# A two-layer state-space kernel: scratch copies in 4 KB pieces, rows of B loaded ahead of C, product 3 of the second scan on POOL, and two statistics moved on DVE

## The chip, the cores and the metric

The kernel runs on one core of one Trainium2 chip. The metric is the device time of one execution in microseconds. A profiled execution comes with a trace: every instruction of TensorE (PE, with its weight loads PEld), VectorE (DVE), ScalarE (ACT) and GpSimd (POOL), the DMA issues of SyncE (SP) and POOL, and the clock granted to TensorE. All data is float32.

## The reference

Four stages, each `x = layernorm(x + f(x))`, on 4096 tokens of 256 channels. The first `f` is a Mamba-2 layer (chunked scan), the second a small coupling network applied three times. The change lies mostly in the third and fourth:

```
xz = x @ w_in.T + b_in;  x_ssm, z = split(xz);  z = silu(z)
dt = softplus(x_ssm @ w_dt.T + b_dt)
Bm, Cm = x_ssm @ w_B.T + b_B, x_ssm @ w_C.T + b_C          # 16 states each
A = -exp(A_log)                                            # (256 channels, 16 states)
for each token t, channel d, state n:
    h[d,n] = exp(A[d,n] * dt[t,d]) * h[d,n] + dt[t,d] * Bm[t,n] * x_ssm[t,d]
    y[t,d] = sum over n of h[d,n] * Cm[t,n]
y = ((y + D * x_ssm) * z) @ w_out.T + b_out
x1 = layernorm(y + x) * gamma + beta;  x = layernorm(x + x1)
h = layernorm(x) * ln_gamma + ln_beta
x = layernorm(x + x + 0.5 * (silu(h @ w1 + b1) @ w2 + b2)) # w1, w2 from integers times scales
```

The text of the reference writes the last two lines with `residual = x`; the kernel joins the normalizations into scales and shifts, which is why there are "norm 3", "norm 4 and 5" and "norm 6".

## The kernel before, in words

**Stages.** Up to some 330 us runs the Mamba-2 layer, up to some 520 us the coupling network, and then the scan stage, which is the third and the fourth stage together. Tokens are worked in 8 blocks of 512. In the scan stage channels lie on the 128 partitions, two tiles of 512 tokens side by side (2 x 512 elements a partition).

**One state of one block** takes these steps (`n` is the state, 0 to 15; `k` the half of the channels):
- SP loads row `n` of B (`load_B`, L1620) and of C (`load_C`, L1626) from the scratch tensor `CB_rows`, spread over all partitions: 256 KB in pieces of 2 KB. There are four buffers for each. The loads wait for an earlier use of their buffer.
- POOL multiplies `dt*x` by the row of B (`into`, L2560; "input n" in the text).
- ACT makes the decay `exp(A*dt)` in PSUM, once for each half (`decay`, L2021).
- DVE runs the scan over 512 tokens, once for each half (`scan`, L2343).
- ACT saves the last column for the next block (`carry`, L2032) and copies the row of C into a PSUM bank, of which there is one (`spread_C`, L2027). DVE multiplies state and C (`product`, L2350). For the states in `on_pool` (0, 12 and 14) POOL multiplies instead, straight from the loaded row (L2570), and ACT makes no copy.
- PE transposes the product and adds it up over the states (`add_up`, L1762).

**Order.** Each engine works through a list written out by hand, one iteration `it` for each block, with the names `cur` (block `it`), `post` (`it-1`), `last` (`it-2`), `old` (`it-3`). DVE scans states 8 to 15 of a block in the iteration after the one that scans 0 to 7. Semaphores alone tie the engines together; an instruction that waits holds all behind it on its engine. SP's list holds the loads too: a load that waits holds the ones behind it.

**Between the scans** the same lists hold the rest of the blocks before: the gated output is transposed and projected; DVE adds the residual `x2` to it (`residual`, L2362) and takes statistics (`stats3`, L2369, two halves); POOL turns them into scale and shift (`norm3`, `norm36`, L2592 and L2600; `norm36` does norm 6 of an older block with it); ACT applies them; POOL multiplies by gamma (`scaled`, L2632) and adds `x2 + beta` (`summed`, L2637); DVE takes the second statistics (`stats4`, L2374); POOL makes norm 4 and 5 of them (`norm45`, L2605); ACT applies them; PE and ACT run the two layers of the feed-forward network. `x2 + beta` is made by a DMA of POOL that adds beta, spread over partitions, onto the buffer of `x2` (`shifted`, L2577). ACT also prepares the next block: `evac_x`, `evac_d` and, behind the decays of states 8 and the first of 9, `soft_step` (L2056), which needs another function table.

**Scratch.** The second stage stores its result twice, as tokens (`x2_tokens`, L1094) and as channels (`x2_rows`, L1103); the scan stage loads blocks of them again (`load_x2`, L1607, and `load_xT`, L1602), and `load_x2` stands on SP behind B 2. The token form moves in pieces of 1 KB, the channel form in pieces of 2 KB; beta moves in pieces of 1 KB.

Of the kernel before, what the change touches and what calls it, by code (L numbers as in the profile page):

```python
# [43 lines left out]
def build(nc, d, out, scratch):  # L44
    with ExitStack() as ctx:
# [967 lines left out]
        x2_tokens, x2_rows = scratch["x2_tokens"].rearrange("(n p) f -> p n f", p=P), rows(scratch["x2_rows"])  # L1013
# [7 lines left out]
        def coupling():  # L1021
# [66 lines left out]
            def sync(e, early_loads):  # L1088
# [3 lines left out]
                for b in range(NB):  # L1092
                    e.wait_ge(c_n, 4 * b + 4)
                    e.dma_start(x2_tokens[:, b * NC:(b + 1) * NC, :], x2s[b % 2][:, :, :]).then_inc(c_tok[b % 2], DMAS)  # L1094
# [8 lines left out]
                    e.dma_start(x2_rows[:, :, tokens(b)], x1T[:, :, tokens(b)]).then_inc(c_row, DMAS)  # L1103
# [424 lines left out]
        with ExitStack() as pd:  # L1528
# [12 lines left out]
            beta_row = d["everywhere"].rearrange("(a o n) -> a o n", a=1, o=1)[:, :, sum(n for _, n in EVERYWHERE) - DM:]  # L1541
# [34 lines left out]
            p_g, on_pool = d_sem("p_g"), (0, 12, 14)  # L1576
# [24 lines left out]
            def sync(e):  # L1601
                def load_xT(b):  # L1602
                    e.wait_ge(pe_z, 2 * b)
                    e.wait_ge(c_row, DMAS * (b + 1))
                    e.dma_start(xT[:, :, :], x2_rows[:, :, b * TB:(b + 1) * TB]).then_inc(ld_xT, DMAS)

                def load_x2(b):  # L1607
# [6 lines left out]
                    e.dma_start(x2, x2_tokens[:, b * NC:(b + 1) * NC, :]).then_inc(ld_x2, DMAS)  # L1614
# [34 lines left out]
                for it in range(NB + 3):  # L1649
                    old, post, cur, nxt = it - 3, it - 1, it, it + 1  # L1650
                    if live(post):
# [7 lines left out]
                        load_C(post, 13)  # L1659
                    if 0 < cur < NB:  # L1660
                        store_CB(cur)
# [8 lines left out]
                    if live(post):  # L1670
                        load_x2(post)
# [10 lines left out]
                    if live(cur):  # L1682
# [4 lines left out]
                        load_B(cur, 7)  # L1687
                        load_C(cur, 6)
                        load_B(cur, 8)
                        load_C(cur, 7)  # L1690
                        load_B(cur, 9)
                        load_C(cur, 8)
                        load_B(cur, 10)
# [326 lines left out]
            def scalar(e):  # L2020
# [130 lines left out]
                for it in range(NB + 3):  # L2151
# [124 lines left out]
                    if live(cur):  # L2276
                        decay(cur, 4, 1)
                        spread_C(cur, 3)
# [63 lines left out]
            def vector(e):  # L2342
# [116 lines left out]
                for it in range(NB + 3):  # L2459
# [4 lines left out]
                    if live(post):  # L2464
                        scan(post, 8, 0)
# [3 lines left out]
                    if live(post):  # L2469
                        product(post, 7)  # L2470
# [46 lines left out]
                    if 0 <= post < NB - 1:  # L2517
                        residual(post, 1)
                        stats3(post, 0)
                    if live(cur):  # L2520
                        scan(cur, 3, 0)
                        scan(cur, 3, 1)
                    if 0 <= post < NB - 1:
                        stats3(post, 1)
                    if live(cur):
                        product(cur, 2)
                    if live(cur):
                        scan(cur, 4, 0)
                        scan(cur, 4, 1)
                        product(cur, 3)  # L2530
# [28 lines left out]
            def pool(e):  # L2559
# [17 lines left out]
                def shifted(b):  # L2577
                    e.wait_ge(v_pre, 2 * b + 2)
                    e.dma_start(x2, beta_row.to_broadcast([P, NC, DM]), accum_op=ALU.add).then_inc(ld_beta, DMAS)
# [209 lines left out]
```

## Time and profile before

| | us |
|---|---|
| median of 3 runs | 1088.25 |
| lowest, highest | 1087.13, 1093.55 |
| profiled execution, its own time | 1091.2 |
| span of its trace | 1089.2 |
| busy PE, PEld, DVE | 980.9, 743.0, 929.0 |
| busy ACT, POOL | 839.4, 709.3 |
| granted TensorE clock, mean | 0.966 |

The page cuts the span into 40 equal slices of 27.2 us and gives the busy share of each in tenths:

```profile
DVE  7999999999963797865799898999999899999751
POOL 2556566766761111223789899999999899999530
PEclk9999999999998999999877799999999999999999
DMA  6543435433415002112998968588786978678301
```

The scan stage begins in slice 20. A row of the time line gives start, duration, engine, line, operation, what is written and read, and in brackets the idle time before it with its releaser. Neighbouring starts on DVE lie closer than the durations say, since an instruction starts while the one before it drains.

### The profile page before, as it was taken

How to read it: one execution, taken by the hardware profiler on the slowest of the kernel's cores; microseconds unless marked ns; L12 is line 12 of the kernel's file. 1: busy time of each engine (PE TensorE's matmuls, PEld its weight loads, DVE VectorE, ACT ScalarE, POOL GpSimd, SP SyncE). 2: the span in 40 equal slices, each digit the busy share in tenths (PEclk: the TensorE clock that was granted, in tenths of full speed). 3: DMA queues.
4: the chain of work that ended last, by engine and by line, in shares of the span. 5: the costliest groups of instructions: out<-in, count | busy, mean ns of one | idle time of the engine just before them, and what ended most of it. 6: DMA issues, size and time to landing. Idle time of an engine off the chain costs nothing. (4 is left out here: it accounts for less than half of the span.)

```text
span 1089.2 us, 17899 instructions
## 1 busy us (share of the span) xinstructions
PE 980.9 (90%) x5612; PEld 743.0 (68%) x5612; DVE 929.0 (85%) x1234; ACT 839.4 (77%) x1633; POOL 709.3 (65%) x603
## 2 busy tenths in 40 slices
PE   6999999999978999998668499999999989997987
PEld 4777777777754555555446387777778777886776
DVE  7999999999963797865799898999999899999751
ACT  7778878878746668767877789898998988987733
POOL 2556566766761111223789899999999899999530
PEclk9999999999998999999877799999999999999999
DMA  6543435433415002112998968588786978678301
GB/s 178 145 134 116 135 110 141 122 99 111 126 46 195 0 1 75 43 39 85 244 163 185 141 152 183 129 199 158 162 169 162 168 133 192 171 146 170 86 1 39
DMA packets 97617, 137.53 MB, mean 126 GB/s; under 512 B 8818, under 2 KB 52338, under 8 KB 97524
## 3 DMA queue, kind: packets, MB, share of 16 engines
q1 hardware_dynamic: 93828, 132.73, 50.2%
q0 software_dynamic: 3696, 3.67, 2.8%
q8 instruction: 45, 0.74, 0.3%
q14 instruction: 48, 0.39, 0.2%
HBM read 120.12 MB, written 14.16 MB: 123 GB/s over the span
## 5 line engine op out<-in xcount | busy, mean ns | idle before, releaser
L2348 DVE TENSOR_TENSOR_SCAN oa<-bank_a,h,oa 128x512 f32<-128x512 f32 x128 | 159.8, 1269 | 13.6 <-ACT h L2034 9.7
L2348 DVE TENSOR_TENSOR_SCAN ob<-bank_a,h,ob 128x512 f32<-128x512 f32 x128 | 160.0, 1268 | 8.0 <-ACT bank_a L2025 4.5
L1830 PE MATMUL bank_m<-w,f_h 128*128 128x256 f32 x448 | 104.4, 383 | 0.0
L1491 POOL TENSOR_TENSOR oa<-ob,x1T 128x1024 f32<-128x1024 f32 x8 | 18.8, 2355 | 130.5 <-DVE ob L1391 130.5
L2025 ACT ACTIVATE bank_a<-s,A 128x512 f32<-128x512 f32 x128 | 86.7, 683 | 21.2 <-DVE oa L2348 15.1
L2025 ACT ACTIVATE bank_a<-dtc,A 128x512 f32<-128x512 f32 x128 | 87.0, 684 | 13.7 <-DVE oa L2348 8.1
L1830 PEld LDWEIGHTS bank_m<-w,f_h 128*128 128x128 f32 x448 | 84.4, 192 | 14.1 <-issue 3.6
L1770 PE MATMUL bank_y<-ident,ob 128*128 128x128 f32 x512 | 71.7, 286 | 23.2 <-DVE ob L2354 11.8
L1770 PE MATMUL bank_y<-ident,oa 128*128 128x128 f32 x512 | 72.3, 288 | 17.7 <-DVE oa L2354 17.6
L1770 PEld LDWEIGHTS bank_y<-ident,ob 128*128 128x128 f32 x512 | 62.7, 148 | 34.5 <-DVE ob L2354 14.5
L2568 POOL TENSOR_TENSOR ob<-s,Bb 128x1024 f32<-128x1024 f32 x32 | 76.1, 2378 | 15.0 <-DMA Bb<-CB_rows 10.9
L1770 PEld LDWEIGHTS bank_y<-ident,oa 128*128 128x128 f32 x512 | 63.0, 149 | 29.1 <-DVE oa L2354 21.2
L2568 POOL TENSOR_TENSOR ob<-uc,Bb 128x1024 f32<-128x1024 f32 x32 | 76.1, 2377 | 10.2 <-DMA Bb<-CB_rows 6.5
L673 DVE TENSOR_TENSOR_SCAN L<-abc,zeros,b_id 128x512 f32<-128x512 f32 x64 | 78.3, 1265 | 4.6 <-POOL xd L883 3.6
L2568 POOL TENSOR_TENSOR oa<-uc,Bb 128x1024 f32<-128x1024 f32 x32 | 76.1, 2378 | 9.0 <-DMA Bb<-CB_rows 4.4
L883 POOL TENSOR_TENSOR xd<-xs,L 128x512 f32<-128x512 f32 x32 | 34.0, 1062 | 72.4 <-DVE xs L662 71.9
L2568 POOL TENSOR_TENSOR oa<-s,Bb 128x1024 f32<-128x1024 f32 x32 | 76.1, 2377 | 3.3 <-POOL ob L2575 2.1
L2354 DVE TENSOR_TENSOR oa<-ob,bank_c 128x1024 f32<-128x1024 f32 x64 | 77.3, 1207 | 0.9
L2030 ACT ACTIVATE bank_c<-Cb 128x512 f32<-128x512 f32 x104 | 61.6, 592 | 13.2 <-DVE ob L2354 8.2
L334 PE MATMUL b_op<-W_out,zs 128*128 128x256 f32 x256 | 63.1, 389 | 0.0
L2575 POOL TENSOR_TENSOR ob<-oa,Cb 128x1024 f32<-128x1024 f32 x24 | 57.2, 2383 | 2.7 <-PE bank_y L1770 2.7
L640 DVE SCALAR_TENSOR_TENSOR b_p<-raw,columns,b_p 128x512 f32<-128x512 f32 x72 | 54.2, 753 | 3.3 <-ACT b_p L465 1.7
(405 smaller groups left out, 2912.7 us busy)
## 6 DMA issues: line engine op xcount, KB each, us to landing
Bb<-CB_rows SPq DMA_DIRECT2D x128, 256.0 KB, 6.6
Cb<-CB_rows SPq DMA_DIRECT2D x128, 256.0 KB, 6.4
abc<-decays SPq DMA_DIRECT2D x32, 512.0 KB, 4.5
Ebc<-ramps SPq DMA_DIRECT2D x64, 128.0 KB, 3.1
uT<-in_uT SPq DMA_DIRECT2D x8, 512.0 KB, 4.2
u<-in_u SPq DMA_DIRECT2D x8, 512.0 KB, 3.9
x_tokens<-x2s SPq DMA_DIRECT2D x8, 512.0 KB, 3.2
x_rows<-x1T SPq DMA_DIRECT2D x8, 512.0 KB, 3.0
```

The lines of the kernel that those rows point to most:

```text
L334: i = e.matmul(b_op[:, 0:DM], zs[b % 2][:, m, ts], W_out[:, m, :], start=(m == 0), stop=(m == MD - 1))
L640: e.scalar_tensor_tensor(to, raw[:, m, t:t + TB], cw[:, m, t:t + 1], acc[:, :], ALU.mult, ALU.add).then_inc(v_conv, 1)
L673: e.tensor_tensor_scan(L[:, hs, :].rearrange("p h t -> p (h t)"), abc[g % 2][:, hs, :].rearrange("p h t -> p (h t)"), b_id[:, :], zeros[:, ...
L883: e.tensor_tensor(heads(xd[:, :]), heads(xs[g % 2][:, :]), L[:, :, CH - 1:CH].to_broadcast([P, NH, HD]), ALU.mult).then_inc(p_xd, 1)
L1770: i = e.matmul(p_y[c // 2][:, at:at + P], prod[n % 2][:, k, c * CH:(c + 1) * CH], ident[:, :], start=False, stop=(n == NS - 1), is_transpo ...
L1830: i = e.matmul(to, f_h[:, k, c * CH:(c + 1) * CH], w2[:, k, :], start=False, stop=(c % 2 == 1 and k == KF - 1))
L2025: e.activation(p_a[k][:, :], dtc[b % 2][:, k, :], ACT.Exp, scale=A[:, k, n:n + 1]).then_inc(a_a, 1)
L2030: e.activation(p_c[:, :], Cb[n % 4][:, :], ACT.Copy).then_inc(a_c, 1)
L2348: e.tensor_tensor_scan(s[:, k, :], p_a[k][:, :], s[:, k, :], h0[:, n, k:k + 1], ALU.mult, ALU.add).then_inc(v_s, 1)
L2354: e.tensor_tensor(prod[n % 2][:, :, :], state[(NS * b + n) % 4][:, :, :], both(p_c[:, :]), ALU.mult).then_inc(v_g, 1)
L2568: e.tensor_tensor(state[at % 4][:, :, :], uc[b % 2][:, :, :], both(Bb[n % 4][:, :]), ALU.mult).then_inc(p_b, 1)
L2575: e.tensor_tensor(prod[n % 2][:, :, :], state[(NS * b + n) % 4][:, :, :], both(Cb[n % 4][:, :]), ALU.mult).then_inc(p_g, 1)
```

## The change

- `x2_tokens`, `x2_rows` are laid out by partition and block, so that stores and loads of a block move 4 KB to or from a partition in one piece. Beta is repeated four times in an input of its own (`beta_rows`), so that its load moves 4 KB a partition too.
- On SP `load_x2` goes ahead of the store of B and C of the next block; B 8 goes ahead of C 6, B 9 ahead of C 7, B 10 ahead of C 8.
- State 3 joins `on_pool`: its product goes from DVE (and the copy from ACT) to POOL, between norm 3 and input 6. With it C 7 waits for POOL's product.
- On DVE both `stats4` go ahead of scan 8's first half, and the second `stats3` ahead of both halves of scan 3.
- On POOL `summed` and `norm45` go one input earlier each.

```
-        x2_tokens, x2_rows = scratch["x2_tokens"].rearrange("(n p) f -> p n f", p=P), rows(scratch["x2_rows"])
+        x2_tokens, x2_rows = scratch["x2_tokens"], scratch["x2_rows"]
-   e.dma_start(x2_tokens[:, b * NC:(b + 1) * NC, :], x2s[b % 2][:, :, :]).then_inc(c_tok[b % 2], DMAS)
+   e.dma_start(x2_tokens[:, b, :], x2s[b % 2][:, :, :].rearrange("p c f -> p (c f)")).then_inc(c_tok[b % 2], DMAS)
-   e.dma_start(x2_rows[:, :, tokens(b)], x1T[:, :, tokens(b)]).then_inc(c_row, DMAS)
+   e.dma_start(x2_rows[:, b, :, :], x1T[:, :, tokens(b)]).then_inc(c_row, DMAS)
-   beta_row = d["everywhere"].rearrange("(a o n) -> a o n", a=1, o=1)[:, :, sum(n for _, n in EVERYWHERE) - DM:]
+   beta_row = d["beta_rows"].rearrange("(a n) -> a n", a=1)
-   p_g, on_pool = d_sem("p_g"), (0, 12, 14)
+   p_g, on_pool = d_sem("p_g"), (0, 3, 12, 14)
-   e.dma_start(xT[:, :, :], x2_rows[:, :, b * TB:(b + 1) * TB]).then_inc(ld_xT, DMAS)
+   e.dma_start(flat(xT), x2_rows[:, b, :, :].rearrange("p k t -> p (k t)")).then_inc(ld_xT, DMAS)
-   e.dma_start(x2, x2_tokens[:, b * NC:(b + 1) * NC, :]).then_inc(ld_x2, DMAS)
+   e.dma_start(flat(x2), x2_tokens[:, b, :]).then_inc(ld_x2, DMAS)
@@ SP
                         load_C(post, 13)
+                        load_x2(post)
                     if 0 < cur < NB:
                         store_CB(cur)
...
                         load_B(cur, 2)
-                    if live(post):
-                        load_x2(post)
...
                         load_B(cur, 7)
+                        load_B(cur, 8)
                         load_C(cur, 6)
-                        load_B(cur, 8)
+                        load_B(cur, 9)
                         load_C(cur, 7)
-                        load_B(cur, 9)
+                        load_B(cur, 10)
                         load_C(cur, 8)
-                        load_B(cur, 10)
                         load_B(cur, 11)
@@ ACT
                         decay(cur, 4, 1)
-                        spread_C(cur, 3)
                         carry(cur, 3)
@@ DVE
-                    if live(post):
-                        scan(post, 8, 0)
                     if 0 <= last < NB - 1:
                         stats4(last, 0)
                         stats4(last, 1)
                     if live(post):
+                        scan(post, 8, 0)
                         product(post, 7)
...
                         stats3(post, 0)
+                        stats3(post, 1)
                     if live(cur):
                         scan(cur, 3, 0)
                         scan(cur, 3, 1)
-                    if 0 <= post < NB - 1:
-                        stats3(post, 1)
-                    if live(cur):
                         product(cur, 2)
                     if live(cur):
                         scan(cur, 4, 0)
                         scan(cur, 4, 1)
-                        product(cur, 3)
                         scan(cur, 5, 0)
@@ POOL
-   e.dma_start(x2, beta_row.to_broadcast([P, NC, DM]), accum_op=ALU.add).then_inc(ld_beta, DMAS)
+   e.dma_start(flat(x2), beta_row.to_broadcast([P, NC * DM]), accum_op=ALU.add).then_inc(ld_beta, DMAS)
                     if live(cur):
+                        product(cur, 3)
                         into(cur, 6)
                         into(cur, 7)
                         into(cur, 8)
                     if 0 <= post < NB - 1:
                         scaled(post)
+                        summed(post)
                     if live(cur):
                         into(cur, 9)
                     if 0 <= post < NB - 1:
-                        summed(post)
+                        norm45(post)
                     if live(cur):
                         into(cur, 10)
-                    if 0 <= post < NB - 1:
-                        norm45(post)
-                    if live(cur):
                         into(cur, 11)
@@ inputs and scratch
+        "beta_rows": np.tile(a[L1 + "beta"], NC),
-    ("x2_tokens", (T, DM)), ("x2_rows", (DM, T))
+    ("x2_tokens", (P, NB, NC * DM)), ("x2_rows", (P, NB, KD, TB))
```

## Rows read from the trace of the kernel before

**Rows 1.** Busy us (x instructions) of each engine in one stretch, clock, DMA:
```profile
750.00:825.00 75.00, 70.06 (x422) 57.44 (x422) 72.28 (x73) 67.39 (x123) 70.32 (x43) 1.00 0.82 169
```

**Rows 2.** Time line of DVE: the product of state 9 in blocks 0 to 4
```profile
561.76 1.20 DVE L2354 TENSOR_TENSOR oa<-ob,bank_c 128x1024 f32<-128x1024 f32 x1
...
624.54 1.20 DVE L2354 TENSOR_TENSOR oa<-ob,bank_c 128x1024 f32<-128x1024 f32 x1
...
689.26 1.22 DVE L2354 TENSOR_TENSOR oa<-ob,bank_c 128x1024 f32<-128x1024 f32 x1
...
752.69 1.21 DVE L2354 TENSOR_TENSOR oa<-ob,bank_c 128x1024 f32<-128x1024 f32 x1
...
816.11 1.21 DVE L2354 TENSOR_TENSOR oa<-ob,bank_c 128x1024 f32<-128x1024 f32 x1
```

**Rows 3.** Time line of DVE, block 4: scan 4, product 3, scans 7, 8, statistics, 9
```profile
790.05 2.56 DVE L2348 TENSOR_TENSOR_SCAN oa<-bank_a,h,oa 128x512 f32<-128x512 f32 x2 [1.44 <-ACT h L2034]
792.54 1.20 DVE L2354 TENSOR_TENSOR oa<-ob,bank_c 128x1024 f32<-128x1024 f32 x1
...
803.36 1.28 DVE L2348 TENSOR_TENSOR_SCAN ob<-bank_a,h,ob 128x512 f32<-128x512 f32 x1 [0.35 <-POOL ob L2568]
804.55 1.27 DVE L2348 TENSOR_TENSOR_SCAN oa<-bank_a,h,oa 128x512 f32<-128x512 f32 x1
805.74 1.29 DVE L2376 BATCH_NORM_STATS2 st<-xl 128x6 f32<-128x512 f32 x2
...
811.06 1.28 DVE L2348 TENSOR_TENSOR_SCAN ob<-bank_a,h,ob 128x512 f32<-128x512 f32 x1 [0.54 <-ACT bank_a L2025]
```

**Rows 4.** Time line of ACT, block 4: evac_x, spread_C 4, decays 7 and 9
```profile
792.70 0.69 ACT L2041 ACTIVATE xc<-bank_m,columns 128x512 f32<-128x512 f32 x1 [0.27 <-PE bank_m L40]
...
793.83 0.60 ACT L2030 ACTIVATE bank_c<-Cb 128x512 f32<-128x512 f32 x1 [0.35 <-DVE oa L2354]
...
802.55 0.67 ACT L2025 ACTIVATE bank_a<-dtc,A 128x512 f32<-128x512 f32 x1
...
805.86 0.69 ACT L2025 ACTIVATE bank_a<-dtc,A 128x512 f32<-128x512 f32 x1 [0.18 <-DVE oa L2348]
```

**Rows 5.** Time line of DVE: the second statistics of blocks 0 and 4
```profile
616.36 1.30 DVE L2376 BATCH_NORM_STATS2 st<-xl 128x6 f32<-128x512 f32 x2 [4.85 <-POOL xl L2641]
...
871.75 1.31 DVE L2376 BATCH_NORM_STATS2 st<-xl 128x6 f32<-128x512 f32 x2 [2.50 <-POOL xl L2641]
```

**Rows 6.** Time line of POOL, block 4: input 5, beta's DMA, input 7, sum
```profile
784.09 2.38 POOL L2568 TENSOR_TENSOR ob<-uc,Bb 128x1024 f32<-128x1024 f32 x1 [0.92 <-DMA Bb<-CB_rows]
786.40 1.34 POOL L2579 DMA_DIRECT2D s<-in_everywhere  x1
...
793.90 2.37 POOL L2568 TENSOR_TENSOR ob<-uc,Bb 128x1024 f32<-128x1024 f32 x1 [1.14 <-DVE oa L2354]
...
803.21 2.38 POOL L2641 TENSOR_TENSOR xl<-xl,s 128x1024 f32<-128x1024 f32 x1
```

**Rows 7.** Time line of SP's queue, block 1: the issue of B 9
```profile
597.49 0.79 SPq L1624 DMA_DIRECT2D Bb<-CB_rows  x1
```

**Rows 8.** Time line of POOL, block 1: inputs 3 and 9
```profile
585.87 2.36 POOL L2568 TENSOR_TENSOR ob<-s,Bb 128x1024 f32<-128x1024 f32 x1 [1.40 <-DMA Bb<-CB_rows]
...
611.68 2.34 POOL L2568 TENSOR_TENSOR ob<-s,Bb 128x1024 f32<-128x1024 f32 x1 [3.42 <-DMA Bb<-CB_rows]
```

**Rows 9.** Busy us by stretch, as rows 1; the clock is the third number from the end
```profile
615.00:630.00 15.00, 8.48 (x51) 7.22 (x52) 12.86 (x12) 9.23 (x19) 13.82 (x15) 0.54 0.95 152
```

**Rows 10.** Time line of POOL, block 0: input 6
```profile
541.16 2.39 POOL L2568 TENSOR_TENSOR oa<-uc,Bb 128x1024 f32<-128x1024 f32 x1
```

**Rows 11.** DMA queues from 786 to 800 us: packets, MB, share of 16 engines
```profile
q1 hardware_dynamic: 998, 1.81, 61.7%
q0 software_dynamic: 528, 0.52, 33.7%
```

**Rows 12.** Beta's DMA, all seven: us from its issue to its landing
```profile
DMA to landing us min/median/max: 10.0/11.5/15.9
```

More of the change, by code:

```diff
@@ L1012, in build @@
         ld_B, ld_C = [d_sem(f"ld_B{i}") for i in range(4)], [d_sem(f"ld_C{i}") for i in range(4)]
-        x2_tokens, x2_rows = scratch["x2_tokens"].rearrange("(n p) f -> p n f", p=P), rows(scratch["x2_rows"])
+        x2_tokens, x2_rows = scratch["x2_tokens"], scratch["x2_rows"]
         c_row, c_tok = new_sem("c_row"), [new_sem("c_tok0"), new_sem("c_tok1")]
@@ L1539, in both @@
                 return x.rearrange("p (o t) -> p o t", o=1).to_broadcast([P, KD, TB])
-            beta_row = d["everywhere"].rearrange("(a o n) -> a o n", a=1, o=1)[:, :, sum(n for _, n in EVERYWHERE) - DM:]
+            beta_row = d["beta_rows"].rearrange("(a n) -> a n", a=1)
             def rowwise(v):
@@ L1659, in sync @@
                         load_C(post, 13)
+                        load_x2(post)
                     if 0 < cur < NB:
@@ L1687, in sync @@
                         load_B(cur, 7)
+                        load_B(cur, 8)
                         load_C(cur, 6)
-                        load_B(cur, 8)
+                        load_B(cur, 9)
                         load_C(cur, 7)
-                        load_B(cur, 9)
+                        load_B(cur, 10)
                         load_C(cur, 8)
-                        load_B(cur, 10)
                         load_B(cur, 11)
@@ L2469, in vector @@
                     if live(post):
+                        scan(post, 8, 0)
                         product(post, 7)
@@ L2519, in vector @@
                         stats3(post, 0)
+                        stats3(post, 1)
                     if live(cur):
@@ L2701, in pool @@
                     if live(cur):
+                        product(cur, 3)
                         into(cur, 6)
                         into(cur, 7)
-                    if live(cur):
                         into(cur, 8)
@@ L2707, in pool @@
                         scaled(post)
+                        summed(post)
                     if live(cur):
@@ L2778 @@
         "columns": np.concatenate([column(down[n]) for n, _ in COLUMNS], axis=1),
+        "beta_rows": np.tile(a[L1 + "beta"], NC),
         "everywhere": np.concatenate([every[n].reshape(-1) for n, _ in EVERYWHERE]),
@@ L2784 @@
     out = nc.dram_tensor("out", (T, DM), F32, kind="ExternalOutput").ap()
-    scratch = {n: nc.dram_tensor(n, shape, F32, kind="Internal").ap() for n, shape in (("x2_tokens", (T, DM)), ("x2_rows", (DM, T)), ("CB_rows", (2 * NS, T)), ("decays", (NB * NC, DT, CH)), ("ramps", (NB * NC, DT, CH)))}
+    scratch = {n: nc.dram_tensor(n, shape, F32, kind="Internal").ap() for n, shape in (("x2_tokens", (P, NB, NC * DM)), ("x2_rows", (P, NB, KD, TB)), ("CB_rows", (2 * NS, T)), ("decays", (NB * NC, DT, CH)), ("ramps", (NB * NC, DT, CH)))}
     build(nc, dram, out, scratch)
```

26 lines of the change are left out of this document (7 added, 19 removed).

## The prediction

> **What bounds the kernel now.** The page's row of forty slices comes first: DVE stands at 8 to 9 tenths through most of the last half, the scan stage (from 520 us), and every edit but the layout of two scratch stores lies there. In a steady stretch DVE is busy 72.3 us of 75, POOL 70.3 and ACT 67.4 [rows 1]: three engines near full, so a microsecond taken from one counts only if the other two leave room. The pace of a block is read from DVE's product of state 9, which comes once a block: 62.8, 64.7, 63.4 and 63.4 us from one to the next [rows 2]. The third view is DVE, ACT and POOL in order of time through one block. It shows a loop that DVE's busy share hides. The first half of scan 8 ends at 805.8; only then may ACT run the first decay of state 9, and behind that, in ACT's order, stand a table load, the softplus of the next block and another table load. Then comes the second decay of state 9, for which DVE waits 0.54 us at 811.06 [rows 3, 4]. From 805.86 to 811.06 are 5.2 us. The last view is the waits of DVE: for POOL it waits long only twice, 4.85 and 2.50 us, both ahead of the second normalization's statistics [rows 5].
>
> **The sum is made** for the profiled execution, 1091.2 us with a span of 1089.2; the median of the three runs is 1088.25, so 2.95 less.
>
> **Product 3 leaves DVE** in all 8 blocks: 1.20 us by its row, 1.1 from its start to the next [rows 3]; ACT loses the copy of C for it, 0.6 us like the one at 793.83. At most that is 8 x 1.1 = 9 us. How much arrives is read on ACT. The lost copy stood ahead of the second x evacuation, which waits for PE until 792.70 anyway [rows 4], so its removal moves nothing behind that. What ACT gains comes later: the copy of C 4 no longer waits 0.35 us for product 3. From there ACT runs without a gap through both norms and the decays to that of state 7 at 802.55, which the scan at 803.36 has to have [rows 3, 4]. So I take 0.45 us a block, the copy moving from 793.83 to 793.38; the ends are 0 and 1.1.
>
> **Product 3 enters POOL** behind the first norm, 2.38 us. It waits for nothing there: scan 3 is over by 787.4 (790.05 less the wait of 1.44 and product 2), and POOL is at this point at 790.4 (793.90 less 1.14 and one input of 2.35). The 1.14 us that POOL waited for product 3 ahead of input 7 [rows 6] go away. The sum ahead of input 9 takes 2.33 us from the way to the second statistics, what the product puts in. POOL ended the sum at 805.6 (803.21 + 2.38); less 1.14 that is 804.45, and less the wait of 0.92 for a row of B [rows 6], if it goes, 803.5. DVE would be done with scan 7 at 804.05 (805.74, less scan 8's 1.2, less 0.45). So both arrive together, and I take 0.2 us of new waiting, in one block; the second norm then ends before input 10, which is wanted 3 us later still.
>
> **Statistics ahead of scan 8.** Both, 1.2 us, now delay the first half of scan 8 and with it the whole ACT loop of 5.2 us. DVE filled that loop with the statistics, product 7 and two scans (4.7 us); now with 3.5. The wait at 811.06 grows by 1.2. Against it stands the 0.45: **+0.7 us in a steady block**. If ACT gains nothing it is +1.2, if all 1.1 arrive +0.1. The last block has no softplus behind it: -0.5. The other pair of statistics goes ahead of scan 3; ACT is late there until 790.05 by 1.44 us [rows 3] whatever DVE's order, so that costs 0, and 0.6 if this cover were gone.
>
> **B ahead of C, x2 earlier.** C 7 now waits on SP for POOL's product 3 (end 792.8); behind it stand B 10, C 8, B 11, the output store and C 9. B 10 and B 11 must wait for inputs 6 and 7 in any case (795.1 and 797.5), and are used only behind the sum: free. B 9 comes ahead of C 7 and leaves when input 5 ends (786.4), 6 us earlier. In block 1 B 9 left at 597.49 [rows 7] and input 9 began at 611.68 after 3.42 us of idle [rows 8]: 14.1 us of landing. Issued at 595.5 it is there at 609.6, before it is wanted. The x2 load, put where SP waits for ACT anyway, clears the way for B 3, which cost 1.40 us [rows 8]. POOL then ends block 1's sum at 612.5 (616.36 less 3.42 and, in part, 1.40 with beta's landing), but now the ACT loop follows that the stall had hidden: second half of scan 9 at 612.5 + 2.4 + 5.2 = 620.1, was 616.36 + 4.7 = 621.1. That is -1.0 and not -4.9. Block 5 in the same way: 867.6 + 2.4 + 5.2 = 875.2, was 871.75 + 4.7 = 876.5: -1.3.
>
> **Clock.** Behind the 4.85 us stall PE was granted 0.54 of full speed from 615 to 630, near its 1.2 GHz level [rows 9], and block 2 took 64.7 us where 63.4 are usual [rows 2]. With a shorter stall I expect it to stay up: block 2 is -1.3 + 0.7 = -0.6; the other end is +0.7.
>
> **Block 0** has no normalization yet, and POOL is just ahead of DVE. Input 6 starts at 541.16 [rows 10], and behind product 3 at 543.5; scan 6 follows 1.3 us later than today. +1.3, at the low end 0.
>
> **4 KB pieces.** The loads of x2 and xT and the two stores are off the path. Of the beta load the row shows 528 pieces, 0.52 MB, that hold 33.7% of the engines' 14 us, while 998 pieces and 1.81 MB of the other queue hold 61.7% [rows 11]: 4.7 us of all 16 engines, at the other queue's bytes per time 2.5. It leaves at 786.4 and is now wanted at 802.1, 15.7 us later; it lands after 11.5 us in the median, 15.9 at most [rows 6, 12]. POOL's own 1.34 us to issue it may fall (0 to 1.34 less). I take 0 for all of this, as nothing of it is waited for. The Trainium skill (DMA: Bandwidth & Descriptors, Queues, rings and completion order) says that each DMA engine changes between its queues a packet at a time, by which larger beta packets would push the rows of B back. No run here shows a 4 KB piece yet; by that rule B 8, with 14.2 us to spare, would at the worst landing of 14.1 plus beta's 4.7 be 4.6 us late once, and the sum would come to 1093.
>
> **Sum:** +1.3 (block 0) - 1.0 (1) - 0.6 (2) + 0.7 x 3 (3, 4, 6) + 0.2 - 1.3 (5) - 0.5 (7) = +0.2 us. Forecast: **no change**, 1091.4 for a profiled execution and 1088.5 for the median.
>
> **Rivals.** *A, the loop is not tight.* ACT has some slack behind scan 8 that the order of the rows does not show, and the wait there does not grow. Then the stalls pay in full: +1.3 - 3.9 (1) - 1.8 (2) - 0.5 x 3 - 3.8 (5) - 0.5 (7) = -10.2, so 1078; with the whole 1.1 of each product 1073. For it: DVE is the fullest engine and loses an instruction, and its wait at 811.06 is only 0.54 us. Chance 0.22, of which 0.14 lies beyond 1%.
> *B, the beta load becomes the wait; slower.* The sum now wants beta 15.7 us after its issue, and from that point each microsecond is DVE's, since statistics, scan 8 and the ACT loop stand behind it. The 15.9 us of one landing speaks for it, the median of 11.5 against. With landings of 17.7 us in the 6 middle blocks it costs 6 x 2 = 12: 1100.5. Chance 0.08.
> *C, the loads stay jammed.* Another row comes late in B 9's stead, and blocks 1 and 5 gain nothing, nor does the clock: +1.3 + 0 + 0.7 x 5 - 0.5 = +4.3, so 1092.5. For it: 14.1 us for one row of 256 KB is congestion, not order. Chance 0.16.
> The forecast itself has 0.54.
>
> **Range and chances.** The forecast's own bounds are 4 us to either side: below, ACT lets all of the 1.1 through in 6 blocks; above, it lets nothing through and the clock dips again. With C and the nearer part of A the range is 1077 to 1096; outside lie B and the far part of A. About 1% (11 us) is what a measurement of this kernel can tell from no change: faster 0.14, same 0.78, slower 0.08.
>
> **What would show it.** Right: DVE's wait ahead of scan 9's second half grows from 0.54 to about 1.7; no 4.85 or 2.50 ahead of the statistics; DVE busy 9 to 10 us less, POOL 19 more; steady products of state 9 64.1 us apart. Wrong: that wait still near 0.5 (A); POOL idle ahead of the sum, released by the beta load (B); POOL idle ahead of inputs 6 to 9 for rows of B (C).

## The result, and the profile after

| | before | after |
|---|---|---|
| median of 20 executions each, us | 1091.7 | 1094.38 |
| lowest, highest | 1087.13, 1094.82 | 1091.59, 1097.03 |
| profiled execution: its own time, span | 1091.2, 1089.2 | 1091.81, 1090.0 |
| busy DVE, POOL, ACT | 929.0, 709.3, 839.4 | 920.8, 723.9, 835.0 |

The ratio of after to before is 1.0035, with a 95% interval of 1.0023 to 1.0047: slower by a third of a per cent, well inside 1%, but the interval lies clear of 1. (The ratio is estimated from the single executions; the two medians alone give 1.0025.) DVE lost 8.2 us of work and the kernel gained nothing by it.

The page of the changed kernel, its slices and its DMA queues:

```profile
DVE  7999999999963897965799898999989999999751
POOL 3456466766761111323889999999999999999530
DMA  5443434433415002113996668487676657667201
...
q1 hardware_dynamic: 86788, 132.73, 47.0%
q0 software_dynamic: 1008, 3.67, 1.7%
```

In the last half DVE's slices are much as before, and POOL's are almost all nines: the work that left DVE is on POOL. The answer to [rows 1], the same 75 us:

```profile
750.00:825.00 75.00, 69.01 (x412) 55.88 (x412) 70.66 (x71) 66.13 (x120) 71.08 (x43) 1.00 0.73 170
```

DVE is busy 1.6 us less and POOL 0.8 us more; the DMA share fell from 0.82 to 0.73. Where DVE's time went is seen in block 4, in DVE's time line (the answer to [rows 3]: scans 4 and 7, statistics, scan 8, product 7, scan 9):

```profile
791.00 2.56 DVE L2346 TENSOR_TENSOR_SCAN oa<-bank_a,h,oa 128x512 f32<-128x512 f32 x2 [1.44 <-ACT h L2033]
...
803.84 1.28 DVE L2346 TENSOR_TENSOR_SCAN ob<-bank_a,h,ob 128x512 f32<-128x512 f32 x1
805.03 1.29 DVE L2374 BATCH_NORM_STATS2 st<-xl 128x6 f32<-128x512 f32 x2
806.23 1.27 DVE L2346 TENSOR_TENSOR_SCAN oa<-bank_a,h,oa 128x512 f32<-128x512 f32 x1
807.42 1.21 DVE L2352 TENSOR_TENSOR oa<-ob,bank_c 128x1024 f32<-128x1024 f32 x1
...
812.74 1.28 DVE L2346 TENSOR_TENSOR_SCAN ob<-bank_a,h,ob 128x512 f32<-128x512 f32 x1 [1.75 <-ACT bank_a L2024]
```

and in ACT's, the answer to the last of [rows 4]:

```profile
807.54 0.69 ACT L2024 ACTIVATE bank_a<-dtc,A 128x512 f32<-128x512 f32 x1 [1.39 <-DVE oa L2346]
808.25 1.28 ACT L2057 ACT_TABLE_LOAD   x1
809.55 1.06 ACT L2057 ACTIVATE s<-s 128x1024 f32<-128x1024 f32 x1
810.62 1.28 ACT L2024 ACT_TABLE_LOAD   x1
811.91 0.69 ACT L2024 ACTIVATE bank_a<-dtc,A 128x512 f32<-128x512 f32 x1
```

Scan 8's first half starts at 806.23, behind the statistics. ACT has been idle for 1.39 us for it. Then ACT runs decay, table load, softplus, table load and decay without a gap, and DVE, whose filling is 1.2 us shorter, waits 1.75 us where it waited 0.54. The waits of DVE from 520 us on (total, times, longest) show that this is now the largest within the blocks; only two waits at the very end of the kernel, together 16.8 us and as long before, come to more. Seven of the eight are this wait, one in each of blocks 0 to 6, 1.72 or 1.75 us long; the one in block 0 is as long before the change, and the eighth is one of 0.93 in block 2:

```profile
DVE ob L2346 <- ACT bank_a L2024: 13.2, 8, 1.8
DVE oa L2346 <- ACT h L2033: 9.8, 6, 2.6
```

Block 4 is 64.16 us long by the start of scan 9's second half (748.58 to 812.74), where it was 63.4. What the stalls gave back is seen in block 1 on DVE (the answer to the first of [rows 5]; the second has no wait any more). The statistics there are of block 0's tokens, but they stand in the stretch in which DVE works on states 8 to 15 of block 1, and are called those of block 1 from here on; those of [rows 5] at 871.75 are those of block 5 in the same way:

```profile
612.18 1.30 DVE L2374 BATCH_NORM_STATS2 st<-xl 128x6 f32<-128x512 f32 x2 [2.39 <-POOL xl L2635]
...
619.89 1.28 DVE L2346 TENSOR_TENSOR_SCAN ob<-bank_a,h,ob 128x512 f32<-128x512 f32 x1 [1.75 <-ACT bank_a L2024]
```

The wait for POOL fell from 4.85 to 2.39 us, and the one for ACT's loop, which the long stall had hidden, came behind it. POOL in block 4 (the answer to [rows 6]: beta's DMA, product 3, sum, input 9):

```profile
786.34 0.95 POOL L2573 DMA_DIRECT2D s<-in_beta_rows  x1
...
790.49 2.35 POOL L2569 TENSOR_TENSOR oa<-ob,Cb 128x1024 f32<-128x1024 f32 x1 [0.58 <-PE bank_y L1769]
...
802.37 2.37 POOL L2635 TENSOR_TENSOR xl<-xl,s 128x1024 f32<-128x1024 f32 x1 [0.20 <-POOL xl L2629]
804.70 2.36 POOL L2562 TENSOR_TENSOR ob<-uc,Bb 128x1024 f32<-128x1024 f32 x1
```

The sum ends at 804.7 and DVE begins the statistics at 805.03, without a wait. Beta's DMA takes POOL 0.95 us instead of 1.34, and over its seven issues it lands after 10.1 us at least, 10.8 in the median and 12.2 at most:

```profile
DMA to landing us min/median/max: 10.1/10.8/12.2
```

### The profile page after: what moved, and what is told of

Its sections match the earlier page's. It is cut to its first block and busy times, and to the rows that moved or that the text cites. A ratio compares the mean times of both kernels' runs of the same rounds, so it can differ in the third digit from the quotient of the medians.

```text
span 1090.0 us, 17891 instructions
## 1 busy us (share of the span) xinstructions
PE 979.1 (90%) x5612; PEld 740.8 (68%) x5612; DVE 920.8 (84%) x1226; ACT 835.0 (77%) x1625; POOL 723.9 (66%) x611
## 5 line engine op out<-in xcount | busy, mean ns | idle before, releaser
L1769 PEld LDWEIGHTS bank_y<-ident,oa 128*128 128x128 f32 x512 | 62.8, 149 | 26.2 <-DVE oa L2352 18.1
L2352 DVE TENSOR_TENSOR oa<-ob,bank_c 128x1024 f32<-128x1024 f32 x56 | 67.8, 1211 | 3.5 <-PE bank_y L1769 2.6
L2029 ACT ACTIVATE bank_c<-Cb 128x512 f32<-128x512 f32 x96 | 56.9, 593 | 11.4 <-DVE ob L2352 9.3
```

The costliest lines, as they stand in the source:

```text
L1769: i = e.matmul(p_y[c // 2][:, at:at + P], prod[n % 2][:, k, c * CH:(c + 1) * CH], ident[:, :], start=False, stop=(n == NS - 1), is_transpo ...
L2029: e.activation(p_c[:, :], Cb[n % 4][:, :], ACT.Copy).then_inc(a_c, 1)
L2352: e.tensor_tensor(prod[n % 2][:, :, :], state[(NS * b + n) % 4][:, :, :], both(p_c[:, :]), ALU.mult).then_inc(v_g, 1)
```

## The experiments

"Steady block" is the distance between the same instructions of two neighbouring blocks, 3 and 4 or 4 and 5, on DVE. Before it is 63.4 us, after 64.15. The first four experiments share one set of executions of the kernel before (28), the next four another (26), the last three a third (12). A number in brackets is a number of executions. Steady blocks of one kernel agree within 0.06 us; blocks 0 and 1 don't. The loads alone and the filled loop on top of them have the same order of instructions up to scan 9 of block 1, and the pieces alone and their filled version too. Yet block 0 takes 37.9 and 41.8 us in the first two, and block 1 takes 58.6 and 62.0 in the others. So one profile can't price a change in these two blocks to better than some 3 us.

**Scan 8 first.** The changed kernel, with only the order of scan 8 and the statistics as before:

```
@@ DVE, changed kernel
+                    if live(post):
+                        scan(post, 8, 0)
                     if 0 <= last < NB - 1:
                         stats4(last, 0)
                         stats4(last, 1)
                     if live(post):
-                        scan(post, 8, 0)
                         product(post, 7)
```

> The changed kernel with one edit undone: on DVE the first half of scan 8 stands ahead of the second statistics again. Theory L (the ACT loop from scan 8 through the softplus to scan 9 sets the pace): DVE's wait ahead of scan 9's second half falls from 1.75 back to about 0.55 us, steady blocks take 63.0 us instead of 64.15, and the time is some 7 us below the changed kernel: 1087 to 1088, ratio to before about 0.996. Rival P (POOL with its fourth product is the bound): POOL's work is untouched, so blocks stay at 64.1 and the ratio at 1.0035.

1091.76 us (12 executions) against 1093.32 for the kernel before (28), ratio 0.9988, interval 0.9974 to 1.0003. DVE, then POOL behind the sum, in the steady block:

```profile
810.34 1.28 DVE L2346 TENSOR_TENSOR_SCAN ob<-bank_a,h,ob 128x512 f32<-128x512 f32 x1 [0.55 <-ACT bank_a L2024]
```

```profile
803.55 2.37 POOL L2563 TENSOR_TENSOR ob<-uc,Bb 128x1024 f32<-128x1024 f32 x1
806.50 0.20 POOL L2603 TENSOR_SCALAR ve<-st 128x4 f32<-128x4 f32 x1 [0.58 <-DVE st L2374]
```

The wait for ACT is back at 0.55, so the order of scan 8 and the statistics is what had made it 1.75. But the block is 63.43 us and not 63.0, and the ratio not 0.996 as expected. POOL is now the bound: it is busy 60.56 of 63.43 us, what is left are its own gaps of 0.2 to 0.4 us, and it has a new wait of 0.58 us. With norm 4 and 5 one input earlier, POOL reaches them before DVE has finished the statistics.

**Product 3 back on DVE.** The changed kernel with this one edit undone:

```
-            p_g, on_pool = d_sem("p_g"), (0, 3, 12, 14)
+            p_g, on_pool = d_sem("p_g"), (0, 12, 14)
@@ ACT
+                        spread_C(cur, 3)
@@ DVE
+                        product(cur, 3)
@@ POOL
-                        product(cur, 3)
```

> The changed kernel with product 3 back on DVE and its copy back on ACT; the order of the statistics and all loads stay as changed. Theory L: the loop stays and the 0.45 us that the moved product gave each block is lost: blocks of 64.3 to 64.6 us, ratio to before 1.004 to 1.007. Rival P: POOL loses 19 us of work, so blocks fall to 63.4 us and the ratio to 0.998 to 1.000.

1094.37 us (12) against 1093.32, ratio 1.0018, interval 1.0001 to 1.0035. The steady block:

```profile
806.58 1.29 DVE L2375 BATCH_NORM_STATS2 st<-xl 128x6 f32<-128x512 f32 x2
...
814.29 1.28 DVE L2347 TENSOR_TENSOR_SCAN ob<-bank_a,h,ob 128x512 f32<-128x512 f32 x1 [1.75 <-ACT bank_a L2024]
```

The wait is 1.75 us with product 3 on either engine, and the block is 64.62 us against 64.15. So the move of the product is worth 0.47 us a block here, though it takes 1.2 us from DVE. In the whole it is worth nothing that can be told: the ratio of 1.0018 is below the 1.004 to 1.007 that was expected, and the median is 1094.37 us with the product on DVE and 1094.38 with it on POOL. One place where the gain is lost is block 1: with the product on DVE there is no wait ahead of the statistics at 613.23, with it on POOL there is one of 2.39 us.

**The statistics' order alone,** in the kernel before:

```
@@ DVE, kernel before
-                    if live(post):
-                        scan(post, 8, 0)
                     if 0 <= last < NB - 1:
                         stats4(last, 0)
                         stats4(last, 1)
                     if live(post):
+                        scan(post, 8, 0)
                         product(post, 7)
```

> The kernel before with one edit of the change alone: the second statistics ahead of scan 8 on DVE; POOL keeps its order, so its sum ends at the old place, 1.1 us after DVE is ready for the statistics. Theory L: 1.2 us from the longer loop plus 1.1 us of waiting for the sum, some 2.3 us in each of 6 blocks: blocks of 65.7 us, ratio about 1.012. Rival P: the order of two short DVE instructions costs nothing that POOL does not hide, ratio 1.000 to 1.001.

1114.17 us (6) against 1093.32, ratio 1.0189, interval 1.0162 to 1.0215. The steady block is 65.69 us. In DVE's time line the second wait is in block 4, and the third belongs to the stall of [rows 5]:

```profile
814.55 1.31 DVE L2376 BATCH_NORM_STATS2 st<-xl 128x6 f32<-128x512 f32 x2 [0.99 <-POOL xl L2640]
...
822.27 1.28 DVE L2348 TENSOR_TENSOR_SCAN ob<-bank_a,h,ob 128x512 f32<-128x512 f32 x1 [1.75 <-ACT bank_a L2025]
...
884.01 1.31 DVE L2376 BATCH_NORM_STATS2 st<-xl 128x6 f32<-128x512 f32 x2 [3.01 <-POOL xl L2640]
```

This order costs 2.3 us a block by itself: 1.2 in ACT's loop, and 1.0 because the sum on POOL is not ready when DVE wants it. The steady block came as expected; the whole was more than the expected 1.012. Part of that is that a wait for POOL ahead of the statistics is now paid in full, since the loop stands behind it: block 5 takes 69.5 us and not 65.4. Another 3.4 us of this profile are in block 0, where this edit moves nothing; its cause is open.

**All edits of the loads alone,** in the kernel before: 4 KB pieces, `load_x2` earlier, rows of B ahead of C.

```
@@ SP, kernel before with the pieces of 4 KB
+                        load_x2(post)
...
+                        load_B(cur, 8)
                         load_C(cur, 6)
-                        load_B(cur, 8)
+                        load_B(cur, 9)
                         load_C(cur, 7)
-                        load_B(cur, 9)
+                        load_B(cur, 10)
...
```

> The kernel before with the transfers' part alone: the 4 KB pieces, the x2 load earlier, rows of B ahead of C. Theory D (order and pieces end the two stalls): the waits of 4.85 and 2.50 us for the sum go to 1 and 0 us, the rest of the blocks stays at 63.4 us; against the profiled execution of before that is 6 us less, against a median whose runs may have had smaller stalls 2 to 6: ratio 0.994 to 0.998. Rival N (the loads were hidden, the stalls a matter of the execution): ratio 1.000 within 0.001, stalls somewhere else.

1088.37 us (11) against 1093.32, ratio 0.9955, interval 0.9940 to 0.9971. The steady block is 63.41 us as before, and the stall of block 1 is nearly gone:

```profile
613.61 1.32 DVE L2375 BATCH_NORM_STATS2 st<-xl 128x6 f32<-128x512 f32 x2 [0.42 <-POOL xl L2640]
```

The loads, with their pieces, are the useful part of the change.

**The pieces alone,** in the kernel before: the layout of the two scratch tensors and of beta, SP's order untouched (the listing is cut to the loads of `x2` and beta).

```
-   e.dma_start(x2, x2_tokens[:, b * NC:(b + 1) * NC, :]).then_inc(ld_x2, DMAS)
+   e.dma_start(flat(x2), x2_tokens[:, b, :]).then_inc(ld_x2, DMAS)
-   e.dma_start(x2, beta_row.to_broadcast([P, NC, DM]), accum_op=ALU.add).then_inc(ld_beta, DMAS)
+   e.dma_start(flat(x2), beta_row.to_broadcast([P, NC * DM]), accum_op=ALU.add).then_inc(ld_beta, DMAS)
```

> The kernel before with the 4 KB pieces alone; every load stands in its old place. Theory O (the order of the rows ended the stalls): input 9 of blocks 1 and 5 still waits 1 to 3 us for its row of B, DVE still waits 1 to 5 us for the sum there, ratio 0.999 to 1.000. Theory S (the size did it, as beta and x2 hold the DMA engines for a shorter time): no wait above 1 us for the sum, ratio 0.9955 as with both.

1088.21 us (11) against 1091.44 (26), ratio 0.9964, interval 0.9947 to 0.9981. Block 1 on DVE, and POOL's input 9 and sum ahead of it:

```profile
611.45 1.32 DVE L2376 BATCH_NORM_STATS2 st<-xl 128x6 f32<-128x512 f32 x2
```

```profile
606.71 2.36 POOL L2568 TENSOR_TENSOR ob<-s,Bb 128x1024 f32<-128x1024 f32 x1
609.03 2.36 POOL L2641 TENSOR_TENSOR xl<-xl,s 128x1024 f32<-128x1024 f32 x1
```

POOL goes from input 9 to the sum with no wait for a row of B, with B 9 still behind C 7 on SP. Its issue, the answer to [rows 7]:

```profile
597.38 0.71 SPq L1624 DMA_DIRECT2D Bb<-CB_rows  x1
```

It landed 7.4 us after this; issued at 597.49 in the kernel before, it took 14.0. The size of the pieces ended the stalls, not the order of the rows. Block 5's stall is gone too. Which of the three it was, beta, `x2` or the channel form, was not tried one by one. The profiled execution, 1085.25 us, was among the quickest of its eleven, so its gain of 6 us is not the kernel's.

**Scan 8 first, norm 4 and 5 where they were.** The first experiment, and on POOL:

```
@@ POOL, on top of "scan 8 first"
+                    if live(cur):
+                        into(cur, 10)
                     if 0 <= post < NB - 1:
                         norm45(post)
                     if live(cur):
-                        into(cur, 10)
                         into(cur, 11)
```

> The kernel with scan 8 ahead of the statistics (e1), and on POOL the second norm behind input 10 again, where it was before the change. In e1 blocks took 63.4 us with POOL never idle but for waits on the statistics of up to 0.6 us. Theory W (the loop is gone and POOL, which waits for the statistics inside its own chain, is the next bound): that wait goes, blocks take 62.9 to 63.0 us, the 1.68 us ahead of scan 10 in the last block goes as well, and the time is 3 to 6 us below e1: ratio to before 0.993 to 0.996. Rival P (POOL's pure work is the bound): blocks stay at 63.4 and the ratio at 0.998 to 0.999.

1088.29 us (10) against 1091.44, ratio 0.9972, interval 0.9958 to 0.9986: a smaller gain than the 0.993 to 0.996 that was expected, though the steady block is as expected, 62.98 us. POOL no longer waits for the statistics:

```profile
805.97 2.37 POOL L2563 TENSOR_TENSOR oa<-uc,Bb 128x1024 f32<-128x1024 f32 x1
808.43 0.20 POOL L2603 TENSOR_SCALAR ve<-st 128x4 f32<-128x4 f32 x1
```

Against the loads alone (63.41) this is 0.43 us a block for product 3, with the earlier sum and `stats3` that go with it. What it gained there it lost in the first blocks: statistics of block 1 at 615.0 with a wait of 1.14 us, where the loads alone have 613.61 and 0.42.

**The loop filled,** with all edits of the loads in the kernel before. DVE gets the feed-forward's last sums of an older block ahead of the instruction that waits for ACT:

```
@@ DVE, kernel before with the loads
-                        scan(post, 9, 1)
-                        product(post, 8)
                     if 0 <= old < NB - 2:
                         second(old, 0)
+                    if live(post):
+                        scan(post, 9, 1)
+                        product(post, 8)
```

> The kernel before with the transfers' part (e4), and on DVE the first half of the feed-forward sum (two instructions, 0.8 us) moved from behind product 8 to between the two halves of scan 9, where DVE waits 0.54 us for ACT. Theory L: the wait is filled, blocks take 62.9 us and not 63.41, the time is some 2.5 us below e4: ratio to before 0.993. Rival: the instruction now waits for PE's down projection, or ACT is the bound all round, and blocks stay at 63.4 with the ratio at 0.9955.

1086.42 us (5) against 1091.44, ratio 0.9949, interval 0.9930 to 0.9969. Only the steady block shows the gain over the loads alone; the ratios, 0.9949 and 0.9955, can't be told apart. The wait of 0.54 is gone and the steady block is 62.76 us, 0.65 less and a little better than expected:

```profile
807.40 1.26 DVE L2347 TENSOR_TENSOR_SCAN ob<-bank_a,h,ob 128x512 f32<-128x512 f32 x1
808.57 0.84 DVE L2381 SCALAR_TENSOR_TENSOR x3b<-xl,twice,bank_m 128x256 f32<-128x256 f32 x2
809.34 1.27 DVE L2347 TENSOR_TENSOR_SCAN ob<-bank_a,h,ob 128x512 f32<-128x512 f32 x1
```

**The two together:** scan 8 first, norm 4 and 5 later, product 3 on POOL, and the loop filled with the same edit.

> e5 and the filled loop together: product 3 on POOL, scan 8 ahead of the statistics, second norm behind input 10, the feed-forward sum inside scan 9. Theory W: DVE alone would allow 62.5 us, POOL's own work 62.8 to 62.9, so blocks take about 62.9 us and little is left of the filled loop: within 1 us of e5. If DVE or ACT were still the bound: 62.4 to 62.5 us, some 3 us below e5.

1087.44 us (11) against 1091.44, ratio 0.9962, interval 0.9947 to 0.9977. Without the filled loop it was 1088.29, so this is within the 1 us that was expected. The steady block is 62.93 us, 0.17 more than with product 3 left on DVE. POOL is busy 60.56 us of it, with gaps of 0.2 to 0.4 us between dependent steps, and DVE, which has room now, waits for POOL's input instead:

```profile
772.74 1.28 DVE L2346 TENSOR_TENSOR_SCAN ob<-bank_a,h,ob 128x512 f32<-128x512 f32 x1 [0.87 <-POOL ob L2564]
```

So product 3 on POOL is worth 0.47 or 0.43 us a block while ACT's loop binds DVE, and less than nothing once it doesn't. That is read from the steady blocks; the whole times of the last two kernels (0.9962 and 0.9949) can't be told apart.

**Pieces and filled loop, without the order of the loads,** the same edit on the pieces alone:

> Before with the 4 KB pieces alone, and the second half of scan 9 with product 8 behind the feed-forward's sums, so that DVE has work while ACT is in its loop. Theory S (the size of the pieces ended the stalls, the order of the loads adds nothing): steady blocks 62.8 us apart, no wait over 0.4 us ahead of scan 9's second half, no stall over 0.5 us ahead of the second statistics, ratio to before 0.992 to 0.996, the same as with x2 and the rows of B moved too. Theory O (the order is needed as soon as DVE is quicker): blocks of over 63.0 or a stall of over 1 us for POOL ahead of the second statistics, ratio 0.996 or more.

1085.67 us (8) against 1091.72 (12), ratio 0.9945, interval 0.9923 to 0.9967, with steady blocks of 62.76 us and no stall ahead of the second statistics of block 1. Theory S holds, but for a wait of 0.54 us ahead of scan 9's second half in block 1. It beats both kernels with SP's order unchanged. By the whole times neither the pieces alone (0.9964) nor the version with the reordered loads (0.9949) can be told from it.

**Both kernels once more,** unchanged, for a second profile of each.

> The changed kernel once more, for a second profile; its first profiled execution (1091.8 us) was among its quickest. Theory V (what makes most executions slower lies in single stalls of blocks 0 to 2 and in the clock there): steady blocks again 64.15 us apart, and any difference to the first profile lies between 520 and 690 us. Theory U (the steady blocks differ from one execution to another): blocks of 64.3 us or more if this execution takes 1094 us or more.

> The kernel before once more, for a second profile. Theory V: steady blocks again 63.4 us apart, and a difference to the first profile of 1 us or more lies in the stalls ahead of the second statistics of blocks 0 and 4 (4.85 and 2.50 us) and in block 2 behind them. Theory U: steady blocks differ by 0.2 us or more.

The changed kernel took 1092.99 us, the kernel before 1090.92. Of the kernel before, the two stalls of [rows 5] in this execution:

```profile
617.88 1.30 DVE L2376 BATCH_NORM_STATS2 st<-xl 128x6 f32<-128x512 f32 x2 [4.13 <-POOL xl L2641]
...
871.62 1.30 DVE L2376 BATCH_NORM_STATS2 st<-xl 128x6 f32<-128x512 f32 x2 [0.80 <-POOL xl L2641]
```

Steady blocks are again 63.4 and 64.15 us. The stalls of before are 4.13 and 0.80 us instead of 4.85 and 2.50; its scan stage began 1.4 us later (521.47 against 520.08), which took back most of the 1.7 us gained in block 5. In block 1 the shorter stall gave nothing: it takes 63.0 us and not 62.8. Of the changed kernel, the statistics of block 1 come 1.2 us later (613.41 against 612.18) with the same wait of 2.39; 0.4 of that is a later start of the stage (520.44 against 520.03), which block 0 nearly makes up (scan 9's second half at 559.07 against 558.93); the rest, 1.1 us, lies in block 1. Theory V holds for both, but for that start of the kernel before, which comes from ahead of its scan stage.

## Why the prediction was right, step by step

**The whole.** Forecast was no change, +0.2 us for the profiled execution; measured are +0.6 there, +2.1 between the second pair of profiles and +2.7 between the medians. "Same" was right, and the sign of the small remainder was positive as the sum had it. But the slowing is real (the interval begins at 1.0023, 2.5 us), and that the sum came so near in the first pair is partly luck. Here are its terms beside both pairs, block by block from one start of scan 9's second half to the next:

| us | forecast | first pair | second pair |
|---|---|---|---|
| start of the scan stage | 0 | 0.0 | -1.0 |
| block 0 | +1.3 | +0.7 | +0.5 |
| block 1 | -1.0 | -1.9 | -1.0 |
| block 2 | -0.6 | +1.4 | +1.3 |
| blocks 3, 4 and 6 | +2.1 | +2.2 | +2.2 |
| new wait ahead of the statistics | +0.2 | 0 | 0 |
| block 5 | -1.3 | -1.3 | +0.5 |
| block 7 and what follows | -0.5 | -0.4 | -0.4 |
| together | +0.2 | +0.7 | +2.1 |

Block 2 came 2.0 us worse than forecast, blocks 0 and 1 together 1.5 us better in the first pair. And block 5's gain hung on a stall that was 2.50 us in the profile from which the prediction was made and 0.80 in the next one. The forecast for the median, 1088.5 us, started from three executions; twenty gave 1091.7 for the same kernel, and the changed one came to 1094.38.

**Statistics ahead of scan 8: right.** The wait was to grow from 0.54 to about 1.7, and is 1.75; steady products of state 9 were to be 64.1 us apart, and are 64.15; the loop, from ACT's first decay of state 9 to scan 9's second half, was 805.86 to 811.06 and is 807.54 to 812.74, 5.2 us in both. The order alone costs 2.3 us a block, of which the other edits on POOL cover 1.0 (product 3 back on DVE 64.62 us, loads alone 63.41).

**Product 3: right in the steady block.** 0.45 us of its 1.1 were to arrive; 0.47 do, and by the way that was named. ACT in block 4, the copy of C 4 and the decay of state 7:

```profile
794.32 0.59 ACT L2029 ACTIVATE bank_c<-Cb 128x512 f32<-128x512 f32 x1
...
803.03 0.68 ACT L2024 ACTIVATE bank_a<-dtc,A 128x512 f32<-128x512 f32 x1
```

The copy starts 3.3 us behind scan 4 (791.00), where it started 3.8 behind it, ACT runs without a gap from there to the decay, and the scan at 803.84 follows the decay. One step failed: product 3 was to wait for nothing on POOL, and waits 0.58 us for PE. DVE was to be busy 9 to 10 us less and is 8.2; POOL 19 more and is 14.6. The term itself, 8 products of 2.37 us, is 19.0; most of the rest is the pieces', which make POOL's work 3.8 us less by themselves (705.5 us busy in the kernel with the pieces alone), 7 x 0.4 of it at the issue of beta's DMA. The new wait of 0.2 us ahead of the statistics didn't come: POOL was done 0.3 us before DVE.

**Rival A** (loop not tight) is out by the 1.75, rival B by beta's landing of 12.2 us at most, with no wait for it. Rival C is out for block 5 and half out for block 1: B came in time, 2.39 us of the stall stayed. There POOL itself is late. It runs from 564 to 612 us without a wait for a row, and has as much work ahead of the sum as before (product 3 came, input 9 went behind it). DVE, which has neither product 3 nor scan 8's first half to do ahead of the statistics any more, is ready for them at 609.8 us, where it was ready at 611.5.

**Blocks 1 and 5.** Block 1 was to gain 1.0 and gained 1.9 and 1.0, block 5 was to gain 1.3, and gained 1.3 and lost 0.5. The reason given for it, that the ACT loop follows behind the statistics and takes most of the stall back, is seen in block 1: the stall fell by 2.46 us and a wait of 1.75 came. The pieces alone, without the new order, give 4.2 us in block 1 in their profile: there scan 9's second half starts at 558.15 in block 0 and at 616.77 in block 1, before at 558.25 and 621.06. In the profile of the pieces with the filled loop, whose instructions are the same up to there, block 1 takes 62.0 us and gains 0.8. The stall ahead of the statistics is gone in both; what that is worth in block 1 differs from execution to execution.

**What was wrong: the clock.** "With a shorter stall I expect it to stay up: block 2 is -1.3 + 0.7 = -0.6; the other end is +0.7." Block 2 is 1.4 us longer, 2.0 more than predicted and beyond that other end too. The two stretches of 15 us ahead of and behind 615 us, in the kernel before (the second is in [rows 9]), and then in the changed one:

```profile
600.00:615.00 15.00, 7.88 (x38) 4.82 (x36) 11.39 (x10) 13.18 (x24) 11.58 (x6) 0.89 0.83 133
```

```profile
600.00:615.00 15.00, 7.22 (x40) 4.67 (x38) 12.61 (x13) 9.97 (x21) 14.53 (x9) 0.87 0.90 182
615.00:630.00 15.00, 9.63 (x55) 8.27 (x56) 12.47 (x11) 13.28 (x24) 14.09 (x14) 0.56 0.51 146
```

The granted clock is 0.56 in the second stretch, near its lower level of 1.2 GHz, as before, and PE is busy 7 to 8 us of the 15 ahead of it in both. The stall had shrunk to 2.39 us and not gone. The other kernels show what its absence would have given. Of the eight whose stall ahead of the statistics of block 1 is 1.2 us or less, PE is busy 8.5 to 12.2 us in the first stretch and granted 0.56 to 0.77 in the second (pieces alone 0.77, loads alone 0.66, product 3 back on DVE, with no stall, 0.56). Of the five with a stall of 2.4 us or more it is 0.50 to 0.56. So the dip is mostly deeper with a long stall, but comes without one too. A likely reason, not tested, is that PE has less to do in block 1, where no feed-forward of an older block runs yet.

Nor was the clock all of the 1.3 us by which block 2 is longer than a steady block. DVE at scan 4 of block 2, in the kernel before and in the changed one:

```profile
663.66 2.57 DVE L2348 TENSOR_TENSOR_SCAN oa<-bank_a,h,oa 128x512 f32<-128x512 f32 x2 [2.58 <-ACT h L2034]
```

```profile
662.80 2.56 DVE L2346 TENSOR_TENSOR_SCAN oa<-bank_a,h,oa 128x512 f32<-128x512 f32 x2 [2.56 <-ACT h L2033]
```

This wait is 1.44 us in a steady block and 2.56 to 2.60 in block 2 of all 13 profiles, while the granted clock is 1.00 from 645 to 675 us in both kernels. So some 1.1 of the 1.3 us were not the clock's to give back. With the loads alone, where the stall is 0.42 us and the clock 0.66, block 2 still takes 64.95 us between the products of state 9; it is shortest, 63.84, in the pieces alone at 0.77. What the dip itself costs was not isolated. Another part of block 2's miss is that in the kernel before the loop was slack there, 0.18 us of waiting and not 0.54, so that the wait grew by 1.57.

**What was wrong: the pieces.** "I take 0 for all of this, as nothing of it is waited for." The pieces alone make the kernel faster by 0.36%, and end both stalls that the prediction had put down to the order of the loads. Nothing waits for these transfers, but the rows of B share the DMA engines with them. The queues between 786 and 800 us in the changed kernel, the answer to [rows 11] (packets, MB, share of 16 engines):

```profile
q1 hardware_dynamic: 1115, 2.03, 58.8%
q0 software_dynamic: 144, 0.52, 18.9%
```

Beta's bytes are the same, in 144 packets and not 528, and hold 18.9% of 14 us instead of 33.7: 2.6 us of all 16 engines and not 4.7; the prediction's estimate had been 2.5. Over the whole kernel a row of B lands in 5.8 us in the median, where it took 6.6, and in 6.1 with the pieces alone. Rows of B issued in this stretch landed after 4.4 us in the median, where they had taken 7.9. That mixes in the new order, and one of the three, issued 0.1 us behind beta's DMA, took 8.9; with the pieces alone, in the old order, the rows of this stretch landed after 5.5 us in the median. The rule of the Trainium skill cited in the prediction (DMA: Bandwidth & Descriptors, Queues, rings and completion order) is that each DMA engine changes between its queues a packet at a time. The prediction took from it that larger packets on one queue would push the other queue back, and that the sum would be 1093 (4.6 us on top of 1088.5). With the pieces alone these landings got shorter, and in the changed kernel no wait of POOL for a row of B is over 0.7 us from 690 us on, so that price was not paid. The packets beside them were larger, but fewer and over sooner. Another rule of the Trainium skill (Perfetto Trace Analysis, DMA Optimizations) says that transfers under 2 KB carry a significant overhead each, and gives the step from 2 to 4 or 8 KB as an example; the runs agree: the pieces alone gained 0.36% of the whole kernel, with steps from 1 and from 2 KB to 4 KB together.

**Block 0** was to cost 1.3 and cost 0.7 and 0.5: product 3 delayed input 6 by 1.9 us, from 541.16 to 543.02, but POOL's waits for rows of B behind it, 1.02, 0.52 and 0.55 us in the kernel before, absorbed most of it.

**Open.** Why the scan stage starts between 518.7 and 521.5 us in the profiles of kernels whose stages ahead of it differ at most in two scratch layouts. Why block 0, from the start of the stage to scan 9's second half, takes 38 to 39.5 us in nine of the 13 profiles and 41.5 to 42 in the other four. The single executions of one kernel differ by up to 8.5 us, and only profiled ones show where.

## What to carry to other kernels

Before work is moved to another engine, find the loop between engines that sets the pace and ask what fills its wait: here taking 1.2 us of filling out of a 5.2 us loop cost 1.2 us a block, more than the 0.47 that the move of a 1.2 us product gave, and 0.84 us of other work put into it gave 0.65. A stall seen in one profile is a sample: the 2.50 us counted on here was 0.80 in the next. A transfer that nobody waits for has a price where others wait for the same DMA engines; look at its packets and its share of the engines, not at its readers. And try the parts of a bundle one by one: of this one, the pieces gave 0.36% and the rest took back more.

## What the runs showed of the hardware that was not expected

- The same 0.5 MB of an accumulating DMA held the 16 engines 4.7 us in 1 KB pieces and 2.6 us in 4 KB pieces, and cost POOL 1.34 and 0.95 us to issue.
- TensorE's clock dipped between 615 and 630 us in all 13 profiles, to 0.50 to 0.77, with and without a stall of DVE ahead of it.
- B 9 of block 1 landed 14.0 us after its issue, which looked like a question of the order in the queue. With SP's order unchanged and only the pieces of other transfers larger, it landed after 7.4 us and POOL did not wait for it.
